# A gated cross-attention and expert kernel: all of x is loaded first, its statistics are spread over the preparation, and the router-key products move behind the first scores

## The reference, cut to what matters

```python
def _proj(x, W1, b1, W2, b2):
    h = jnp.einsum('bsd,od->bso', x, W1) + b1
    return jnp.einsum('bsd,od->bso', h, W2) + b2
# cross attention: q = layernorm(x), k = v = ctx
qk = einsum('bqd,bkd->bqk', _proj(q), _proj(k)) / sqrt(256) + mask
x = x + tanh(g_xattn) * einsum('bqk,bkd->bqd', softmax(qk), ctx)
# experts: h = layernorm(x), 8 experts, the best one for each token
route = softmax(h @ router_w + router_b)
e = argmax(route); y = (silu(h @ w1a[e]) * (h @ w1g[e])) @ w2[e]
x = x + tanh(g_ffn) * max(route) * y
```

## Time and profile before

| | |
|---|---|
| median of 3 runs | 471.89 us |
| the profiled execution | 472.45 us |
| its span, first to last instruction | 470.6 us |
| mean granted TensorE clock | 0.929 of full speed |
| PE busy | 417.4 us, 89% of the span |
| DVE, ACT, POOL busy | 224.9, 183.6, 247.2 us |
| HBM traffic | 95 GB/s over the span |

### The profile page before, as it was taken

How to read it: one execution, slowest core, us unless ns; L and a number is a source line. 1 busy time by engine, 2 the same in 40 slices (tenths; PEclk the granted TensorE clock), 3 DMA queues, 4 the chain that set the end, 5 groups by cost and what they waited for, 6 DMA issues and landing times.

```text
span 470.6 us, 9969 instructions
## 1 busy us (share of the span) xinstructions
PE 417.4 (89%) x2465; PEld 360.0 (77%) x2466; DVE 224.9 (48%) x533; ACT 183.6 (39%) x355; POOL 247.2 (53%) x318
## 2 busy tenths in 40 slices
PE   5887897134899999999999999999999999999990
PEld 4786874034688888888888898888888888889880
DVE  3479897691244444354444444354434444344430
ACT  1246561060355345444543335434523443323220
POOL 0325995261268567788776226756772577222221
PEclk9959895557799999999999999999999999999996
DMA  7940223540023314423344011430341001100100
GB/s 211 378 137 0 95 96 124 162 168 12 22 90 137 112 26 161 163 115 112 122 186 138 23 34 69 154 118 18 129 174 55 15 23 31 37 23 20 30 23 21
DMA packets 25689, 44.25 MB, mean 94 GB/s; under 512 B 4217, under 2 KB 21421, under 8 KB 23631
## 3 DMA queue, kind: packets, MB, share of 16 engines
q1 hardware_dynamic: 19935, 34.56, 21.1%
q0 software_dynamic: 3456, 9.24, 6.0%
q10 hardware_dynamic: 2288, 0.33, 0.4%
HBM read 35.57 MB, written 8.95 MB: 95 GB/s over the span
## 4 chain that ended last, share of the span: by engine, by line
PE 83%; DVE 8%; DMA 3%; issue 2%; POOL 1%; ACT 1%; POOLq 0%; DVEq 0%; SPq 0%; ACTq 0%
PE pa L1062 21%; PE pg L1062 21%; PE py L1080 21%; PE ph L1072 6%; PE ps_s L993 3%; PE px L1049 3%; PE ps_s L1035 2%; DVE x_row L707 2%; PE ps_xt L902 1%; PE ps_o L1002 1%; DMA ctx_in<-in_ctx 1%; DVE bn L715 1%; DMA residual_rows<-x_row 1%; PE ps_p L930 1%; DMA x_sorted<-residual_rows,idx_now 1%
## 5 line engine op out<-in xcount | busy, mean ns | idle before, releaser
L860 DVE TENSOR_TENSOR ht_lo<-ph,ht_hi 128x512 fp32r<-128x512 f32 x70 | 48.4, 692 | 134.0 <-ACT ht_hi L593 134.0
L458 POOL TENSOR_TENSOR w_lo<-staging,w_hi x84 | 106.9, 1301 | 4.6 <-ACT w_hi L614 3.7
L593 ACT CAST ht_hi<-ph 128x512 fp32r<-128x512 f32 x70 | 41.2, 588 | 121.4 <-PE ph L1072 66.1
L1080 PE MATMUL py<-w_hi,ht_hi 128*128 x280 | 82.0, 293 | 0.9 <-DVE out_tile L868 0.9
L1080 PE MATMUL py<-w_hi,ht_lo 128*128 x280 | 79.2, 283 | 0.0
L1080 PE MATMUL py<-w_lo,ht_hi 128*128 x280 | 79.1, 282 | 0.0
L1062 PE MATMUL pa<-w_hi,xt_hi 128*128 (+1 forms) x140 | 58.7, 419 | 1.7 <-DVE xt_lo L848 1.7
L440 POOL DMA_INDIRECT x_sorted<-residual_rows,idx_now x37 | 39.3, 1061 | 31.1 <-POOL idx_now L438 31.1
L1062 PE MATMUL pg<-w_lo,xt_hi 128*128 (+1 forms) x140 | 55.5, 397 | 0.0
L1062 PE MATMUL pa<-w_lo,xt_hi 128*128 (+1 forms) x140 | 55.4, 396 | 0.0
L1062 PE MATMUL pg<-w_hi,xt_hi 128*128 (+1 forms) x140 | 55.4, 396 | 0.0
(11 more groups left out here) (171 smaller groups left out, 620.2 us busy)
## 6 DMA issues: line engine op xcount, KB each, us to landing
staging<-in_L_ffn_w SPq DMA_DIRECT2D x24, 1024.0 KB
residual_rows<-x_row SPq DMA_DIRECT2D x8, 532.0 KB, 3.7
x_all<-in_x SPq DMA_DIRECT2D x8, 512.0 KB, 9.5
x_sorted<-residual_rows,idx_now POOLq DMA_INDIRECT x37
out<-out_tile,idx_now POOLq DMA_INDIRECT x35, 2.5
x_row<-in_L_xattn_W SPq DMA_DIRECT2D x2, 256.0 KB, 4.6
ctx_in<-in_ctx SPq DMA_DIRECT2D x1, 308.0 KB
mask_in<-in_fside_1xSxS ACTq DMA_DIRECT2D x1, 308.0 KB, 13.5
```

What stands on the lines that cost most here:

```text
L458: lo = nc.gpsimd.tensor_tensor(out=w_lo[:, bass.ds(dst + q * QW, QW)], in0=staging[:, bass.ds(src + q * QW, QW)], in1=w_hi[:, bass.ds(dst ...
L593: nc.scalar.copy(ht_hi[:, j], ph[j][:]).then_inc(hhi_ready[j], 1)
L860: nc.vector.tensor_tensor(out=ht_lo[:, j], in0=ph[j][:], in1=ht_hi[:, j].bitcast(FP32), op=ALU.subtract).then_inc(hlo_ready[j], 1)
L1080: last = mm(py[:, 0:D], ht[:, j, c * P:(c + 1) * P], w[:, bass.ds(slot + (DC * PW + (j * HC + c) * D), D)], start=j == 0 and n == 0, stop= ...
```

## The change

SP issues all eight x groups before the first weight piece. VectorE does `stats1` of groups 0 to 4 (EARLY = 5) inside the preparation, between the copies out of PSUM, whose order changes as well; the other three follow in the loop, one in each of the iterations 0, 1 and 2. POOL does `norm1` for one group at a time. PE does the 16 router-key products after `transpose_tokens(1)` in iteration 0, and its waits for bias, values and router values move to the iterations that need them.

```diff
+        EARLY = 5
-            for g in range(4):
+            for g in range(NG):
                 sp.dma_start(x_all[:, g, :, 0:D], x_groups[g]).then_inc(x_loaded[g], 16)
...
-                for g in range(4 + 2 * k, min(6 + 2 * k, NG)):
-                    sp.dma_start(x_all[:, g, :, 0:D], x_groups[g]).then_inc(x_loaded[g], 16)
...
-            norm1(0, 1)
-            norm1(1, 2)
+            for g in range(EARLY - 1):
+                norm1(g, g + 1)
             mask1(0)
             mask1(1)
+            norm1(EARLY - 1, EARLY)
             for i in range(NG + 2):
                 if 2 <= i + 1 < NG:
                     mask1(i + 1)
-                if 2 * i + 4 <= NG:
-                    norm1(2 * i + 2, 2 * i + 4)
+                if i < NG - EARLY:
+                    norm1(EARLY + i, EARLY + i + 1)
...
+            nc.vector.tensor_copy(keys_t[:, :, :, KEYS:KW],
+                                  router_c[:].unsqueeze(2).to_broadcast([P, DC, B, E])).then_inc(keys_ready, 1)
             stats1(0)
+            stats1(1)
             (bq, bq_wide)
+            stats1(2)
             (kp_t[1])
-            (m_c), stats1(1)
             (values)
-            (router columns of keys_t), (bias_c)
+            (m_c), stats1(3)
             (keys_t[1])
-            (router values)
+            (bias_c), stats1(4)
...
+                if i == 0:
+                    router_values()
-                if i < 3:
-                    stats1(2 * i + 2)
-                    stats1(2 * i + 3)
+                if i < NG - EARLY:
+                    stats1(EARLY + i)
...
             pe.wait_ge(router_c_ready, 1)
             transpose_tokens(0)
-            (16 router-key products, vr_psum)
...
             pe.wait_ge(keys_ready, 3)
-            pe.wait_ge(bias_ready, 1)
-            pe.wait_ge(values_ready, 1)
-            pe.wait_ge(vr_ready, 1)
             for i in range(NG + 2):
+                if i == 1:
+                    pe.wait_ge(bias_ready, 1)
                 if i < NG:
                     scores(i)
                 if i + 1 < NG:
                     transpose_tokens(i + 1)
+                if i == 0:
+                    router_by_keys()
+                if i == 2:
+                    pe.wait_ge(values_ready, 1)
+                    pe.wait_ge(vr_ready, 1)
```

More of the change, by code:

```diff
@@ L650, in _ @@
                                     op=ALU.subtract).then_inc(router_c_ready, 1)
+            dve.wait_ge(router_c_ready, 1)
+            nc.vector.tensor_copy(keys_t[:, :, :, KEYS:KW],
+                                  router_c[:].unsqueeze(2).to_broadcast([P, DC, B, E])).then_inc(keys_ready, 1)
             stats1(0)
+            stats1(1)
             dve.wait_ge(bq_psum, 1)
@@ L655, in _ @@
             nc.vector.tensor_copy(bq_wide[:], bq[:].unsqueeze(2).to_broadcast([P, DC, P])).then_inc(bq_step, 1)
+            stats1(2)
             dve.wait_ge(kp_psum, 1)
             nc.vector.tensor_scalar(kp_t[:, 1], ps_s[0][:, 0:KB], bq[:, 1:2], None, ALU.add).then_inc(kp_ready[1], 1)
-            dve.wait_ge(mc_psum, 1)
-            nc.vector.tensor_copy(m_c[:], ps_o[1][:].rearrange("p (c d) -> p c d", c=DC)).then_inc(mc_ready, 1)
-            stats1(1)
             dve.wait_ge(tanh_ready, 1)
@@ L664, in _ @@
                                     ).then_inc(values_ready, 1)
[L665 to L668, removed]
+            dve.wait_ge(mc_psum, 1)
+            nc.vector.tensor_copy(m_c[:], ps_o[1][:].rearrange("p (c d) -> p c d", c=DC)).then_inc(mc_ready, 1)
+            stats1(3)
             dve.wait_ge(keys_psum, 1)
@@ L671, in _, with router_values @@
                                     None, ALU.mult).then_inc(keys_ready, 1)
-            dve.wait_ge(vr_psum, 1)
-            nc.vector.tensor_scalar(values[:, :, D:XW], ps_l[0:KEYS, 16:16 + B * E].rearrange("p (b e) -> p b e", b=B),
-                                    tanh_g[0:KEYS, 0:1], None, ALU.mult).then_inc(vr_ready, 1)
+            dve.wait_ge(bias_psum, 1)
+            nc.vector.tensor_scalar(bias_c[:], ps_s[1][:, 0:KB], SCALE, None, ALU.mult).then_inc(bias_ready, 1)
+            stats1(4)
+            def router_values():
+                dve.wait_ge(vr_psum, 1)
+                nc.vector.tensor_scalar(values[:, :, D:XW], ps_l[0:KEYS, 16:16 + B * E].rearrange("p (b e) -> p b e", b=B),
+                                        tanh_g[0:KEYS, 0:1], None, ALU.mult).then_inc(vr_ready, 1)
             def mask_and_max(g):
@@ L955, in _ @@
             transpose_tokens(0)
[L957 to L962, removed]
             for k in range(DC):
@@ L1003, in attend, with router_by_keys @@
                        stop=True).then_inc(attn_psum, 1)
+            def router_by_keys():
+                for b in range(B):
+                    for k in range(DC):
+                        last = mm(ps_l[0:KEYS, 16 + b * E:16 + (b + 1) * E], ctx_t[:, k, b * KEYS:(b + 1) * KEYS],
+                                  router_c[:, k], start=k == 0, stop=k == DC - 1)
+                last.then_inc(vr_psum, 1)
             pe.wait_ge(keys_ready, 3)
-            pe.wait_ge(bias_ready, 1)
-            pe.wait_ge(values_ready, 1)
-            pe.wait_ge(vr_ready, 1)
             for i in range(NG + 2):
+                if i == 1:
+                    pe.wait_ge(bias_ready, 1)
                 if i < NG:
```

## The result

The changed kernel takes 465.61 us (median of 6 runs, 463.41 to 467.68) against 472.0 us for the kernel before (6 runs, 471.44 to 474.92). The ratio is 0.987, with a 95% interval from 0.983 to 0.990: 6.4 us faster. Forecast were 464.7 us and a range from 462.4 to 469.5.

The account below looks back on a forecast made before the run. The prediction took waits on PE, then VectorE, then POOL to bound the attention loop. Gains of 1.75 + 3.1 + 1.7 + 0.65 = 7.2 us took 472.45 to 465.25, at the median 464.7 us, range 462.4 to 469.5.

Parts of the forecast that it names:

- Head: Preparation up to the first mask: key products at 17.7, scores at 21.05, mask at 23.35 instead of 25.13, gain 1.75 us.
- Groups 1 and 2: Attention loop, if PE keeps its clock: first attention add at 33.9 instead of 38.75, 4.85 us, of which 3.1 new.
- these 3.1 us: The new gain in groups 1 and 2, with PE's scores at the high clock and router-key products hidden inside ACT's copy.
- Statistics: One `stats1` in place of two before group 3's mask, 1.7 us; `norm1` of one group in POOL's chain, 0.65 us.
- GpSimd's chain: POOL's work from `norm1` to group 4's mask: 6.45 us instead of 7.1, since `norm1` has one group instead of two.
- the sum: Total gain by the end of the attention loop: 1.75 + 3.1 + 1.7 + 0.65 = 7.2 us.
- Group 3 and group 4: Masks in the attention loop: group 3 at 39.15, gain 6.6 us; group 4 at 45.8 instead of 52.98, gain 7.2 us.
- SP's queue: Loading x groups 4 to 7 ahead of piece 0 costs zero; piece 0 lands at 25.2, its first user comes at 26.8.
- The first, the clock falling again: PE's clock falls at 25 us all the same, for 10 us: gain 3.3 us, 468.6 us; 22 in 100, whole or part.
- The second: The clock stays low beyond that stretch, 3.8 us for each loop group: 472.4 or 476.2 us; 5 in 100.
- third: The loop ends earlier but a later wait takes all the gain: 471.9 us; 3 in 100.
- The fourth: Idle of 44 to 48 us shrinks, no low stretch follows, luckier routing: 1 to 2 us more, 463; within forecast's 67 in 100.

Follow-up runs that it names:

- the pair without the fall: Kernel before, unchanged (472.48 us, ratio 1.001), and changed kernel with the load order of before (465.73 us, ratio 0.985), one profile of each.
- the last run: Idle products in routing and ahead of the first tile, added to the changed kernel with group 7's statistics early and idle head products: 456.85 us, ratio 0.972.

## Why the prediction was right, point by point

**Head.** Right to 0.1 to 0.25 us in the profile: key products at 17.93 for 17.7, scores at 21.12 for 21.05, first mask at 23.44 for 23.35. As a gain it holds where the first rise is alike: 1.7 us with an early rise in both (25.13 to 23.44), 1.9 with a late one (28.03 to 26.13), forecast 1.75. The times themselves are chance: the rise moves the first mask of either kernel by 2.7 to 2.9 us.

**Groups 1 and 2.** The first attention add comes at 33.09 for a forecast 33.9; the scores of 2.0 us at full clock, the products inside the copy and `stats1(5)` are as said. What failed is the step that gives these 3.1 us to the clock. I set them down as scores that take 2.0 us instead of 3.7, and took the clock's fall at 25 us as part of the kernel before. The fall is in part of the executions alone. Between two executions of before without and with it, the loop to group 4 differs by 27.85 − 25.22 = 2.6 us, and the one without it had the later head.

**Statistics.** I counted them as 1.7 and 0.65 us, the third iteration and GpSimd's chain. With full clock from 25 to 35 us in both kernels the loop to group 4 goes from 25.22 to 21.46, so 3.8 us, 1.4 more than I had (the low clock from 48 us in that execution costs group 4 nothing: it comes 7.25 us after group 3, as in the first profile). So of the 3.1 us 1.4 are left, and they belong to the statistics: in the first two iterations VectorE with two `stats1` is itself the bound (a mask each 4.7 to 5.5 us, with no wait ahead of it) as soon as TensorE is fast. Both causes sat on top of each other in the one profile that I had, and the low clock hid the other. Group 4 of the kernel before is masked at 52.98 with the fall and at 53.25 without it, and that is why the sum came out right. In the pair without the fall the missing 1.7 us are half made up by the 0.8 behind group 4, which was no term of the sum. That is luck.

**Group 3 and group 4.** GpSimd's chain: 38.53 to 44.90 is 6.4 us, forecast 6.45. Group 4 at 44.90 for 45.8; the 0.9 us come from the first add. Rhythm 5.1 us after that, as said.

**SP's queue.** Cost zero was right: piece 1 is issued at 23.4 or so (10.03 us for two issues from 13.68), so piece 0 landed there and not at 25.2, and `high0(0)` at 26.28 does not wait. The run with the old load order shows that nothing was gained either.

**Rivals.** The first, the clock falling again, did not come: none of the nine profiles of kernels with the spread statistics has a fall between 25 and 35 us. Of the five with the old statistics two have one and three do not, so its absence in a single profile would have shown little. The Trainium skill's rule on transposes (TensorE: Matmul & The Clock Gate, Part 4: PE-mode transpose) spoke for a fall; this case's trace does not bear it out for this work: the clock held at 1.00 from 25 to 35 us, with PE busy 9.12 of 10 us and transposes among it. What a stretch of transposes alone would do no run here tests. The second and third did not come. The fourth came in part of the executions: PE is busy 2.54 of 4 us from 44 to 48 instead of 0.63, and in the profiles of 463.41 and 463.88 us no low stretch follows up to 62 us; with the old load order and with the products back the clock is at 0.50 for some 3.4 us from 45 us on, and the rhythm stays 5.1. The median is not the 463 of that rival.

**The time.** Loop and head gained 7.9 us to the start of routing in the first two profiles, forecast 7.2, and the medians gained 6.4. The first two profiles happened to have an early rise in both, with the fall in before alone. The pair with a late rise and no fall gained 6.5. The rest of the spread I can't name: with idle products in the head the first mask comes within 0.2 us in three profiles, and the times of the changed kernel with them still lie at 463.5 to 469.6. In the profiles without idle products in routing, the time from its start to the end lies between 383.2 and 385.7 us, and goes with how late the list products and the first tile get the full clock, which is worth 5.5 us in the profile of the last run.

## What to carry to other kernels

One profile can hold two causes on top of each other: ask of a low clock what would bound the stage without it, and look at a second execution before the fall is taken as the kernel's own. Work of an engine that fills gaps elsewhere (here the statistics of x in VectorE's waits of the preparation) is worth what its former place cost under the bound of that place, and a load order is worth something only if a load was late. Work moved into gaps can become the bound of its new place, as here in the head once TensorE runs there at full clock. Where TensorE has nothing to do ahead of a dense stretch, a few idle products can be the cheapest gain in a kernel that is otherwise at its bound, as in routing here. In the head they brought no gain that the times show.

## What the runs showed of the hardware

- The windows of the profile print the granted clock as 1.00 up to its first recorded change, while the matmuls run at half: the same 4 matmuls take 2.40 us at 13.77 in one execution and 1.27 us at 13.02 in another, and the windows print 1.00 for both. In the head the durations tell the clock, not the column.
- With 22 idle products in routing and 20 ahead of the first tile (84 matmuls in all) the 64 list products took 7.69 us for 10.48 and the first tile's matmuls 0.40 us for 0.63, and the part from routing to the end 5.5 us less in the profile.
- Waits of the same length were followed by a fall in one execution and not in another. With the same head, PE waited 1.09 us for the context and W1·W2 behind it took 3.22 us, or it waited 1.02 us and W1·W2 took 1.97. In the first the transposes ahead of the wait had taken 0.84 us, so the clock had risen; in the second they took 1.11 and it rose after them. The changed kernel with PE busy only 1.34 of 3.00 us from 38 to 41 us kept 1.00:

```profile
38.00:41.00 3.00, 1.34 (x7) 0.82 (x6) 2.93 (x15) 1.28 (x7) 2.31 (x4) 1.00 0.00 0
```
